# First unit with experts innermost, its token low halves on GpSimd behind the one-hot rows; units two and four with three experts to a slot tile

## What is computed

```python
probs = softmax(x @ Wr); topk_probs, topk_experts = top_k(probs, 2)
pos = cumsum(onehot) - onehot; keep = pos < capacity   # capacity 40
buf[e, b, pos] += x_rep * keep
h = relu(einsum('ebnc,ech->ebnh', buf, W1) + b1)
y = einsum('ebnh,ehc->ebnc', h, W2) + b2
out = sum over the 2 picks of y[e, b, pos] * keep * p
```

## Time and profile before

| | |
|---|---|
| median of 3 runs | 192.5 us (192.48 to 194.83) |
| the profiled execution: its own time | 192.46 us |
| its span | 190.6 us |
| TensorE busy | 177.0 us, 93% |
| ScalarE busy | 150.2 us, 79% |
| VectorE busy | 135.2 us, 71% |
| GpSimd busy | 65.9 us, 35% |
| mean granted TensorE clock | 0.991 |

### The profile page before, as it was taken

How to read it: one execution, slowest core, us unless ns; L and a number is a source line. 1 busy time by engine, 2 the same in 40 slices (tenths; PEclk the granted TensorE clock), 3 DMA queues, 4 the chain that set the end, 5 groups by cost and what they waited for, 6 DMA issues and landing times.

```text
span 190.6 us, 5849 instructions
## 1 busy us (share of the span) xinstructions
PE 177.0 (93%) x2233; PEld 140.6 (74%) x2233; DVE 135.2 (71%) x396; ACT 150.2 (79%) x357; POOL 65.9 (35%) x104
## 2 busy tenths in 40 slices
PE   7967998999999989799999999999999999999962
PEld 7964998989779947445646566555699998999952
DVE  1889989997666579995452689768888886704562
ACT  3878978879586678898899988998999577879330
POOL 8855175050000014736647664876700000000000
PEclk9889999999999999999999999999999999999999
DMA  5999920000049999369876938440900008000213
GB/s 137 287 335 328 216 60 0 3 0 3 0 126 171 248 215 279 96 146 270 175 176 157 231 104 217 114 119 5 165 3 0 3 0 161 7 2 3 73 41 110
DMA packets 34283, 22.81 MB, mean 120 GB/s; under 512 B 14248, under 2 KB 31184, under 8 KB 34256
## 3 DMA queue, kind: packets, MB, share of 16 engines
q1 hardware_dynamic: 34112, 22.44, 48.7%
q10 hardware_dynamic: 144, 0.00, 0.0%
HBM read 14.05 MB, written 5.24 MB: 101 GB/s over the span
## 4 chain that ended last, share of the span: by engine, by line
PE 66%; DVE 17%; ACT 5%; issue 4%; SPq 4%; DMA 2%; DVEq 0%; POOL 0%; ACTq 0%; POOLq 0%
PE psB L1012 12%; PE psB L1083 7%; PE psS L1066 5%; PE psB L988 4%; PE psS L915 4%; PE psS L896 3%; PE psS L897 3%; PE psS L898 3%; PE psB L1085 3%; DVE xn L736 2%; SPq L496 2%; PE psB L1094 2%; DMA stack<-qk_parts 2%; PE psB L906 2%; PE psB L955 2%
## 5 line engine op out<-in xcount | busy, mean ns | idle before, releaser
L575 POOL TENSOR_SCALAR_AFFINE_SELECT amat<-amat 128x512 f32<-128x512 f32 x64 | 42.9, 674 | 53.1 <-ACT amat L656 51.4
L656 ACT ACTIVATE amat<-psS 128x768 f32<-128x768 f32 x64 | 48.7, 825 | 4.5 <-PE psS L1068 4.3
L627 ACT ACTIVATE hid<-psS,biasT 128x160 f32<-128x160 f32 x128 | 39.5, 403 | 5.5 <-PE psB L1012 2.8
L1012 PE MATMUL psB<-hid,w 128*128 128x160 f32 x256 | 39.8, 303 | 0.3 <-issue 0.2
L1012 PEld LDWEIGHTS psB<-hid,w 128*128 128x128 f32 x256 | 35.7, 190 | 1.1 <-issue 0.7
L896 PE MATMUL psS<-xe,w 128*128 128x160 f16 x128 | 27.1, 233 | 0.9 <-ACT xe L354 0.8
L898 PE MATMUL psS<-xe,w 128*128 128x160 f16 x128 | 27.1, 233 | 0.0
L897 PE MATMUL psS<-xe,w 128*128 128x160 f16 x128 | 27.1, 233 | 0.0
L1083 PE MATMUL psB<-amat,vst 128*32 128x256 f32 x256 | 20.3, 388 | 0.5 <-POOL amat L575 0.3
L1066 PE MATMUL psS<-stack 64*128 64x256 f16 x128 | 16.3, 277 | 1.6 <-ACT amat L656 0.9
L635 ACT ACTIVATE yT<-psB,biasT 128x160 f32<-128x160 f32 x32 | 12.0, 409 | 6.3 <-PE psB L1012 6.2
(11 more groups left out here) (151 smaller groups left out, 352.3 us busy)
## 6 DMA issues: line engine op xcount, KB each, us to landing
qk_parts<-qk SPq DMA_DIRECT2D x16, 256.0 KB, 4.3
stack<-qk_parts SPq DMA_DIRECT2D x16, 256.0 KB, 4.1
stack<-qk_parts SPq DMA_DIRECT2D x32, 128.0 KB, 4.2
amat<-in_L_ffn_W SPq DMA_DIRECT2D x8, 256.0 KB, 5.5
w<-in_L_ffn_W SPq DMA_DIRECT2D x8, 256.0 KB, 5.4
x<-in_L_attn_hidden_states SPq DMA_DIRECT2D x4, 256.0 KB, 4.4
out<-x SPq DMA_DIRECT2D x8, 128.0 KB, 1.8
amat<-in_L_attn_Wq SPq DMA_DIRECT2D x1, 128.0 KB, 5.4
```

Source lines behind the costliest of these rows:

```text
L575: pool.affine_select(out=d, in_=d, pattern=[[0, 2], [0, 2], [1, P]], compare_op=ALU.is_ge, fill=0.0, base=0, channel_multiplier=-1).then_i ...
L627: ins = act.activation(hid[:, n % 2, c, :], psS[:, wide_slot(s) + c // 2, (c % 2) * GS:(c % 2 + 1) * GS], ACT.Relu, bias=biasT[:, e * HC + ...
L656: act.activation(amat[:, n % A_RING, :, :], psS[:, wide_slot(s):wide_slot(s) + 2, 0:T + P], ACT.Square)\
L1012: ins = mm(bank(s)[:, 0:GS], w2[:, e, c, :], hid[:, n % 2, c, :], start=(c == 0), stop=(c == HC - 1))
```

## The change

1. **Units one and three** (`INNER_UNITS`) lay the slots out with the expert innermost: slot `c*8+e` in place of `e*40+c`. The one-hot instruction then compares `iota_e` with a row of eight keys that repeats, `key` is f16, and all three operands have step 1 innermost. The moves from `dph` and `dpl` read PSUM with a step of 8 elements, `down` writes `yT` with a step of 8 elements, every `yt` waits for all eight `down`, and the mask of `pw` is a small one, `emask`.
2. **Units two and four** put three experts (120 slots) in each tile of 128. `key` becomes `keyt` with nine places, the one-hot instruction has 720 elements, `dph` and `dpl` have 360 columns, and `yt.k` waits for experts up to 3k+2 (before: for those that fill 128(k+1) slots, that is 3, 6 and 7).
3. **The first unit's low parts.** `first` stands ahead of all `w1` in GpSimd's list and waits for all four one-hot rows. The high parts are gathered first: `dph` waits for `first_hi` alone, the four `dpl` follow, and the last of them is moved by VectorE.
4. **The last unit.** `ca` is split by slot tile; each part waits for its own `yl`. Two of the last four stores are issued by ScalarE.
5. The bias loads move from SP's queue to ScalarE's, `pad` and `pm` move later, and the five lists are written in another order throughout. There are 60 warm-up matmuls ahead of the picks (54 before) and 6 between `dph` and `dpl`.

```diff
--- before.py
+++ after.py
@@ -68,6 +68,13 @@
+ON_VECTOR = {("dpl", 0, 0, 3)}
+STORED_BY_SCALAR = {("cb", 1, 1, 1), ("cb", 1, 1, 3)}
+
+INNER_UNITS = ((0, 0), (1, 0))
+E_TILE = P // CAP
+USED = KT * E_TILE * CAP
...
 PE_STAGES = stages("""
-wc rx.0 rx.1 rl.0 rl.1 warm.6.0 warm.30.1 warm.10.2 warm.8.3 bt ps.0.0 dph.0.0.0 dpl.0.0.0 dph.0.0.1 dpl.0.0.1
...
+wc rx.0 rx.1 rl.0 rl.1 warm.8.0 warm.24.1 warm.10.2 warm.8.3 warm.10.4 bt ps.0.0 dph.0.0.0 dph.0.0.1 dph.0.0.2
+dph.0.0.3 warm.6.5 dpl.0.0.0 dpl.0.0.1 dpl.0.0.2 dpl.0.0.3 up.0.0.0 up.0.0.1 down.0.0.0 up.0.0.2 down.0.0.1
...
-        key = sb("key", [P, TT, GB, E])
+        key = sb("key", [P, TT, GB, E], f16)
+        keyt = sb("keyt", [P, GB, TT, KT * E_TILE], f16)
...
+        def first_slot(e):
+            return e // E_TILE * P + e % E_TILE * CAP
+
+        def slots_by_expert(t, l, g):
+
+            if (l, g) in INNER_UNITS:
+                return t.rearrange("p (c e) -> p e c", e=E)
+            return t.rearrange("p (e c) -> p e c", e=E)
...
+            pool.memset(keyt[:, :, :, :], 0.0)
             pool.tensor_copy(iota[:, :], iota_i)
+            pool.tensor_copy(iota_e[:, :, :], iota_i.unsqueeze(2).broadcast_to([P, CAP, E]))
...
                 elif kind == "first":
                     p = s[1]
+                    pool.wait_ge(oh_ready, GB)
                     pool.wait_ge(first_hi, p + 1)
...
-                    act.activation(yT[:, parity(l, g), :, e * CAP:(e + 1) * CAP],
+                    act.activation(yT[:, parity(l, g), :, 0:SLOTS].rearrange("p b (c e) -> p b c e", e=E)[:, :, :, e] if (l, g) in INNER_UNITS
+                                   else yT[:, parity(l, g), :, first_slot(e):first_slot(e) + CAP],
...
+                        if s[1:] in INNER_UNITS:
+                            dve.tensor_tensor(rows[:, :, 0:SLOTS].rearrange("p a (c e) -> p a c e", e=E),
+                                              iota_e[:, :, :].unsqueeze(1).broadcast_to([P, TT, CAP, E]),
+                                              key[:, :, i, :].unsqueeze(2).broadcast_to([P, TT, CAP, E]),
+                                              ALU.is_equal).then_inc(oh_ready, 1)
+                        else:
+                            dve.tensor_tensor(rows.rearrange("p a (k n) -> p (a k) n", n=P)[:, :, 0:E_TILE * CAP].rearrange("p k (e c) -> p k e c", c=CAP),
+                                              iota[:, :].unsqueeze(1).unsqueeze(1).broadcast_to([P, TT * KT, E_TILE, CAP]),
...
-                    if kind == "dph" and s[1:3] == (0, 0):
-                        pe.wait_ge(first_split, i // 2 + 1)
+                    if s[1:3] == (0, 0):
+                        pe.wait_ge(first_hi if kind == "dph" else first_split, i // 2 + 1)
...
-                    pe.wait_ge(y_taken, nth[("down", l, g, min(((k + 1) * P - 1) // CAP, E - 1))] + 1)
+                    last_e = E - 1 if (l, g) in INNER_UNITS else min((k + 1) * E_TILE, E) - 1
+                    pe.wait_ge(y_taken, nth[("down", l, g, last_e)] + 1)
...
                 elif kind == "ca":
-                    pe.wait_ge(yl_ready, nth[("yl",) + s[1:3] + (1,)] + 1)
...
+                    tile = s[3]
+                    pe.wait_ge(yl_ready, nth[("yl",) + s[1:]] + 1)
```

More of the change, by code:

```diff
@@ L122 @@
[L122 to L123 removed]
+rx.0 rx.1 ln1.0.0 ln1.0.1 nm.0.0 w1.0 nm.0.1 bt w1.1 w1.2 dph.0.0.0 dph.0.0.1 dph.0.0.2 dph.0.0.3 dpl.0.0.0
+dpl.0.0.1 dpl.0.0.2 ln1.0.2 ln1.0.3 up.0.0.0 up.0.0.1 down.0.0.0 up.0.0.2 w1.3 w1.4 ex.0.0 down.0.0.1 down.0.0.2
+up.0.0.3 wr w1.5 w1.6 up.0.0.4 up.0.0.5 w1.7 down.0.0.3 up.0.0.6 down.0.0.4 down.0.0.5 up.0.0.7 ex.0.1 wqkv
@@ new lines @@
+dpl.1.0.3 sc.7.5 sc.7.6 sc.7.7 ln1.2.2 up.1.0.0 up.1.0.1 down.1.0.0 oT.6 up.1.0.2 oT.7 ln1.2.3 up.1.0.3
+down.1.0.1 down.1.0.2 down.1.0.3 up.1.0.4 up.1.0.5 up.1.0.6 down.1.0.4 down.1.0.5 up.1.0.7 ex.1.1 down.1.0.6
+down.1.0.7 dph.1.1.0 dph.1.1.1 dph.1.1.2 dph.1.1.3 up.1.1.0 up.1.1.1 yt.1.0.0 up.1.1.2 down.1.1.0 up.1.1.3
+yt.1.0.1 yt.1.0.2 down.1.1.1 up.1.1.4 down.1.1.2 up.1.1.5 down.1.1.3 down.1.1.4 down.1.1.5 up.1.1.6 up.1.1.7
+yt.1.1.0 down.1.1.6 down.1.1.7 yt.1.1.1 yt.1.1.2 yt.1.1.3 cb.1.1.1 cb.1.1.3 sq.1
```

203 lines of the change are left out of this document (111 added, 92 removed).

## The result

The changed kernel takes 196.05 us in the median of 20 runs (194.51 to 198.21), the kernel before 194.49 (192.33 to 195.53, 20 runs). The ratio is 1.0107, with a 95% interval of 1.0071 to 1.0143: some 2.1 us slower, where 1.25 us faster had been forecast. It is worked out from the executions within 1.5% of the lowest of their kernel, so it leaves out the seven of the changed kernel near 198 us; the ratio of the two medians is 1.008. Every kernel of this study, the one before too, has its times in two or three groups (before: 192.2 to 193.9, and 194.3 to 195.5; changed: 194.5 to 195.1, 195.5 to 196.2, and 197.8 to 198.2). So beside each ratio the lowest time is given; over all runs it was 192.2 us before and 194.5 for the changed kernel.

A forecast was written before the change was run, and what follows sets the result against it. TensorE was taken as the bound, busy 177.0 of 190.6 us. Start and picks -0.15, columns +0.55, end -1.2, stores -0.45 sum to -1.25 from 192.46: 191.2 us, range 189.3 to 193.4.

The forecast's parts named there:

- One-hot rows: Units one and three, VectorE: a one-hot instruction takes 0.49 us in place of 0.82, two elements at a time.
- The start: Up to up.0.0.0: sel earlier, but warm-ups and GpSimd's late low parts make up.0.0.0 0.35 us later than 17.89.
- "-0.5" to the picks of unit two: Ahead of ps.0.1: one more down and one yt less fill 0.66 us of TensorE's 0.9 wait; gain 0.5 us.
- Columns: Units two and four gather 360 columns in place of 320, in 32 matmuls on TensorE: +0.55 us.
- Middle at nothing: The middle, where all five lists are re-laid: costed at nothing, each engine's work there being the same.
- The end: Behind the last down: yt.1.1.1 moved and ca split, -1.2 us; last stores on two queues, -0.45 us.
- (e): Rival: clock falls again in the gaps between dph, dpl and up, losing 1.65 us: 192.9; chance 0.07.
- (b): Rival: ScalarE pays for steps of 8, 0.29 a move, 0.14 a yT, unit three 1.1 to 2.3: 192.6; chance 0.15.
- (c): Rival: score loads of batches 3 and 4 wait on SP's queue, stalls up to 2.2 us: 193.4; chance 0.15.

The follow-up runs named there:

- e4: Kernel before with only the new slot layouts, the three yt of unit one behind its last down, and ca split; ratio 1.0103 to before.
- e2: Changed kernel with its start and end, but the lists between the last down of unit one and down.1.1.4 in the old order; ratio 1.0291 to before.
- e7: e6 with the start of the changed kernel as well; ratio 1.0234 to before.
- e5: Kernel before with only yt.0.0.0 moved behind the last down of unit one, no layout changed; ratio 1.0132 to before.
- e6: e5's order, and unit one alone with experts innermost, other units as before; ratio 1.019 to the kernel before.
- e3: Changed kernel with 40 warm-up matmuls ahead of the picks in place of 60; ratio 1.0102 to before.
- e11: e3 with the store qk.0.1.1 ahead of the transpose ot.0.1.0 on SP, as before; ratio 1.0123 to the kernel before.
- e16: e11 with unit three's exp, sm.1.0 and pw.1.0 behind the last scores and the Sqrt table load in unit three; ratio 1.0197 to before.
- e1: Kernel before with only the edits of the end: yt.1.1.1 behind the last down, split ca, two stores on ScalarE, late transpose behind two stores; ratio 0.9938.
- e9: Kernel before with ca split and two of the last four stores on ScalarE, nothing moved; ratio 0.9939 to before, median 191.38 us.
- e12: Changed kernel with 40 warm-ups, ScalarE's split of wqkv moved behind the last yt of unit one; ratio 1.0185 to before.

## Why the prediction was wrong

- **One-hot rows, right.** One takes 0.48 us in the median against the 0.49 forecast, the next starts 0.41 behind it against 0.43, and the four together took 1.70. Two elements at a time holds, as the Trainium skill has it (page "Vector Engine (DVE) Microarchitecture Reference", section 5.1). But faster rows bought 0.3 us at `up.0.0.0` (17.63 in e4 against 17.89; counted from `ps` 0.6), since ScalarE's moves and w1's low parts follow.
- **The start, the right mechanism, mis-sized.** `sel` early, the warm-ups behind it (14.9 against 13.1 us; in e2, with the clock of the kernel before, 12.48 where I had 12.5), GpSimd's low halves late: all as written. `up.0.0.0` was to be 0.35 us later than before. Like for like it is 0.9 later (e2, 18.82 against 17.89) or 1.2 (the profiled executions with the late clock, 21.20 against 20.00). Where the full clock comes early it costs nothing: e7 has it at 17.88. From `ps` to `up.0.0.0` I had 5.7 us and it is 6.2. To the end of the rows (2.2) and of the low halves (2.3) the sum held; the last passage, gather, move and start of `up`, is 1.6 us (19.57 to 21.20) where I had 1.2: four matmuls 0.7, VectorE's move 0.5, and three hand-overs between engines of 0.03 to 0.25.
- **The step that failed: "-0.5" to the picks of unit two.** I read the moved `yt` and `down` as 0.44 and 1.10 us of TensorE's work with which a wait is filled. The wait for `sel` did shrink by 0.3, but `sel` itself came later: `ps.0.1` starts 16.24 us behind `up.0.0.0` in place of 15.66, with 0.66 us more work ahead of it, so the gain there is 0.1 and not 0.5. Behind the last `down` of unit one the kernel then loses 1.2, and the whole passage to unit two grew by 1.1 beyond the columns. I never followed what the layout does to the order behind it: each `yt` brings a relay of about 2 us on VectorE and ScalarE, and late it stands in their lists just where they must empty the gather's banks. The diff stated the cause (every `yt` waits for all eight `down`), and my text mentioned it for no price at all. In the order of the kernel before e5 measures it: 1.7 us with no layout changed; e6 adds 0.7 for the dependence. The list of the changed kernel puts two `yt` together behind the second gather and pays 1.1; that this 1.1 is the same relay is read from its trace (TensorE waits 0.4 for `yT`, VectorE and ScalarE alternate between `yt` and the gather's banks) and not from a run of its own.
- **Columns, right.** +0.55 forecast; a pair now takes 0.31 us in place of 0.27, 32 x 0.017 = 0.54.
- **Middle at nothing, wrong.** It cost 1.0 to the first scores in e3 (the store behind the transpose, e11 gives back 0.9) and 1.1 beyond the columns between `sc.0.0` and `up.1.1.0`. Of that, 0.84 goes away with the exp table load between the scores (e16). The list that I costed at nothing because "the work of each engine is the same" held both.
- **The end, right in sign, too large.** Forecast -1.65, measured -1.0. With the 0.4 that `yt.1.1.1` leaves free ahead of the last `down` it is 1.1 in e1. The split of `ca` does the work (e9, 1.1 behind the last `down` to the last addition); two queues bring 0.2 and not 0.45, since the store takes 0.26 longer to land from ScalarE's queue. The Sqrt table load of `sq.1`, which the new list puts behind the last store, runs for 1.28 us inside that landing and is the last thing in the chain, but costs nothing: from the last addition to the end it is 2.65 us with it and 2.66 in e9 without it.
- **The rivals.** (e) came in some executions, 1.2 us in that of e12 where I had 1.65. (b) was half right: writes +0.14 us as forecast, reads nothing, so that of its 1.1 to 2.3 us in unit three 0.4 to 1.4 is left. The Trainium skill's rule of short lines (page "SBUF — State Buffer", section "Door 1: The DMA port swizzle") agrees for the written `yT`. For PSUM it speaks of matmuls, and ScalarE's read, to which the prediction applied it, shows no such cost. (c) named a queue on SP, the right kind and the wrong batch. That the change could lose by an order that it forbids was no rival of mine.

The sum of what was measured, in an execution with an undisturbed start (e3, 40 warm-ups): start -0.1, passage to unit two +1.1 beyond the columns, columns +0.55, loads +1.0, attention and unit three +1.1, unit four -0.2, end -1.0, together +2.45 us, the difference of the spans 193.1 and 190.6. The timed runs say +2.1, and the lowest times +2.2. With 60 warm-ups and a stretch of low clock among them the start is +0.9 in place of -0.1 (e2), the sum 3.5, and the middle group of the changed kernel, at 196.0, is 3.5 above the lower group of before.

## What to carry to other kernels

Before a layout change, list the orders that it forbids, and price each stage that must move by its whole relay on all engines, at the new place, not by its own time on the bounding engine. A stage that fills a wait is worth keeping where it is: here 0.44 us of work early were 1.7 us late. And take the small edits one by one; the one that split a wait in two (`ca`) was worth the whole gain, and the rest of the change buried it. And where a stage waits for filler work, as `ps` does for the warm-ups, price the filler at the slower of the clocks that its executions show.
